# Where TensorE issues the last four attention products and the output projections of a round

## The chip, the cores and the metric

One core of one Trainium2 chip runs the whole program. The metric is the device time of one execution in microseconds, the median of the runs. One execution was also recorded by the profiler; it lasted 3959.9 us from its first to its last instruction.

## The reference, cut to what matters

The program computes a macaron block on x of shape (8, 512, 256): half a local feed-forward stage (two layers), a global attention with 16 heads, and the local stage again. Each layer of the local stage is, for all 8 sequences:

```python
h = shift_token(x)
q, k, v = split(h @ wqkv)                  # 8 heads of 64
q, k = rotary_xpos(l2norm(q) * qs, l2norm(k) * ksc)
o = local_attention(q, k, v)               # windows of 128, own block and the one before
x = x + o @ wo
h = layernorm(shift_token(x)) * lg + lb
a, g = split(h @ w1 + b1)
x = x + (a * gelu(g)) @ w2 + b2
```

The change concerns only this part.

## The kernel before, in words

**Rounds.** A local stage is called twice (call 0 and call 1). A call has 16 rounds, one for each sequence in the first layer and then in the second. The global attention lies between the calls. Within a round each engine works through a list of steps in a fixed order, written out by hand: `PE_STEPS` for TensorE, `ACT_STEPS` for ScalarE, `DVE_STEPS` for VectorE, `POOL_STEPS` for GpSimd. An engine does its steps strictly in that order and waits on semaphores where a step needs another engine's result. A step with `-` belongs to the previous sequence, one with `+` to the next, so three sequences are interleaved. In the last round of a call the `+` steps fall away; in the first one the `-` steps do.

**TensorE's steps that matter here.** A sequence has eight units of two heads by two query blocks.

- `S0` to `S7` (L1480): scores of a unit, on 64 rows of the array.
- `T0` to `T7` (L1490): the turnings (transposes) of a unit's probabilities into banks TB.
- `A0` to `A7` (L1510): the product of turned probabilities and values of a unit, on 64 columns of the array. `A4` and `A5` fill one bank, `A6` and `A7` the other. `A4` and `A6` are 8 instructions, `A5` and `A7` are 12.
- `W0` to `W3` (L1366 to L1368, `psum<-wo_hi,oT_hi` and its two companions): output projection of one head pair, 12 instructions. `W2` needs the bank of `A4` and `A5` after ScalarE (`O2`, L802) and VectorE (`P2`, L1087) have read it, `W3` likewise `A6`, `A7`, `O3` and `P3`.
- `+q`, `+k`, `+v` (L1366 to L1368, `psum<-wqkv_hi,hT_hi` and companions): the next sequence's projections, 6 instructions a step. `+q0` needs `hT_lo` of VectorE (L1016).
- `+Q`, `+K` (L1469): turnings of the rotated q and k, 4 instructions each.
- `-g`, `-a`, `-w`: the previous sequence's feed-forward products.
- `n0`, `n1` (L1528): turnings of the normalised stream, then `g0`, `a0` and so on.
- `B` (L1427): 48 products with one column each that fold the layer norm's bias into `b1`. Only the first round of each layer in each call has it (four rounds in all). In such a round `+v0` waits until VectorE has added the result to `b1t` (its own step `B`, L977).

**VectorE between W3 and n0.** Its list reads `P3 f1 +rq2 x l B +rk2 +ss2 r +rk3 +rq3 j0 j1 nl0 nl1`. Step `x` (L1096) adds the output projection to the stream and needs all four `W`. `l`, `r` (L1104, L1109) take the statistics, `+rk2`, `+rk3`, `+rq3` (L1027, L1031) rotate q and k of the next sequence, `+ss2` (L1038) sums squares, and `j0`, `j1` (L1122) normalise into `nrm`, which `n0` and `n1` of TensorE need. `L6` (L1084) copies the turned probabilities of unit 6 and frees the bank for `T7`; in the second layer VectorE has two further additions (`F`, L1147) ahead of it.

**Queues.** SyncE issues the DMAs in a fixed order too; the three shift copies of a round (L490 to L492) follow half of step `x`.

Of the kernel before, what the change touches and what calls it, by code (L numbers as in the profile page):

```python
# [14 lines left out]
B, N, D = 8, 512, 256  # L15
# [23 lines left out]


PE_STEPS = ("S0 -a2 -g3 S1 -w0 -g4 S2 -a3 -w1 S3 T0 -w2 T1 -a4 S4 T2 A0 S5 A1 A2 S6 T3 -w3 S7 T4 A3 -w4 +z0 +z1 "
            "-g5 A4 T5 +q0 +k0 A5 T6 -w5 +k1 +q1 T7 W0 +q2 A6 W1 A7 W2 +Q0 W3 B +K0 +k2 +v0 +K1 +Q1 +k3 +q3 +v1 "
            "+Q2 +v2 +v3 n0 n1 +Q3 g0 a0 g1 +K2 a1 g2 +K3").split()


# [1628 lines left out]
```

## Time and profile before

| | |
|---|---|
| median of 3 runs | 3955.74 us (3955.32 to 3961.43) |
| the profiled execution | 3959.9 us |
| TensorE matmul busy | 3751.7 us (95%), 23552 instructions |
| VectorE busy | 2649.7 us (67%) |
| ScalarE busy | 2237.8 us (57%) |
| GpSimd busy | 2192.4 us (55%) |
| mean granted TensorE clock | 0.985 of full |
| TensorE's share of the chain that ended last | 86% |

Busy times of TensorE are modelled from start to end of each matmul, and neighbours overlap. So the distance from one start to the next is the better measure of what a group of matmuls costs. The rows of the trace that matter are in a section of their own below; a row gives start, duration, engine, line, operation, what it writes and reads, and how often it repeats, with the idle time before it in brackets.

### The profile page before, as it was taken

To read this page: it belongs to the slowest core of one execution; us is meant where nothing else is said; L and a number is where in the kernel's file an instruction comes from. 1 tells how busy PE (TensorE), PEld (TensorE's weight loads), DVE (VectorE), ACT (ScalarE), POOL (GpSimd) and SP (SyncE) were. 2 spreads that over 40 slices of the span, in tenths; PEclk is the share of its full clock that TensorE was granted. 3 is DMA by queue.
4 is the path that set the end of the run, shared out by engine and by line. 5 is a ranking of instruction groups with operands and counts; after the bars stand their busy time and mean duration, and the time that the engine had idled before them with its cause. 6 is when DMAs were issued, how large, how long until landed. Compare 5 with 4: busy or idle time off the path is not lost.

```text
span 3959.9 us, 75575 instructions
## 1 busy us (share of the span) xinstructions
PE 3751.7 (95%) x23552; PEld 3069.5 (78%) x23552; DVE 2649.7 (67%) x7350; ACT 2237.8 (57%) x5232; POOL 2192.4 (55%) x2179
## 2 busy tenths in 40 slices
PE   4999999999999799999999999998999999999997
PEld 3777777777777688888888888886777777777776
DVE  6677777777777465555555555656777777767774
ACT  2666665567656455444444444445656765567564
POOL 3465565555555355555555555654555555555553
PEclk8999999999999899999999999999999999999999
DMA  4000001110010100000000010001010011100110
GB/s 142 16 31 28 19 19 53 48 36 24 30 31 29 46 28 22 1 17 7 12 17 2 17 44 1 17 1 52 20 35 22 19 41 50 39 30 24 34 32 25
DMA packets 119063, 114.72 MB, mean 29 GB/s; under 512 B 13181, under 2 KB 116233, under 8 KB 118793
## 3 DMA queue, kind: packets, MB, share of 16 engines
q1 hardware_dynamic: 118792, 111.44, 8.9%
q8 instruction: 131, 2.15, 0.2%
q14 instruction: 140, 1.14, 0.1%
HBM read 73.69 MB, written 29.36 MB: 26 GB/s over the span
## 4 chain that ended last, share of the span: by engine, by line
PE 86%; DVE 6%; issue 3%; ACT 2%; POOL 1%; DMA 1%; DVEq 0%; SPq 0%; ACTq 0%; POOLq 0%
PE psum L1366 21%; PE psum L1367 20%; PE psum L1368 20%; PE psum L1480 6%; PE psum L1490 5%; PE psum L1510 4%; PE psum L1469 3%; PE psum L1615 3%; PE psum L1563 1%; DVE probs L1065 1%; PE psum L1446 1%; PE psum L1427 1%; DVE turned_sin L1031 1%; DVE nT_lo L1127 1%; DVE ssq L1038 1%
## 5 line engine op out<-in xcount | busy, mean ns | idle before, releaser
L685 POOL TENSOR_TENSOR ge_lo<-ge,ge_hi 128x512 fp32r<-128x512 f32 x512 | 716.8, 1403 | 541.2 <-PE psum L1368 311.3
L885 ACT ACTIVATE ge<-psum 128x512 f32<-128x512 f32 x512 | 306.3, 598 | 623.7 <-PE psum L1615 611.8
L645 POOL TENSOR_SCALAR probs<-probs,rz 128x256 f32<-128x256 f32 (+1 forms) x1024 | 446.1, 456 | 354.6 <-DVE rz L1079 354.6
L1256 DVE CAST ge_hi<-ge 128x512 fp32r<-128x512 f32 x512 | 245.2, 480 | 537.5 <-ACT ge L885 531.4
L791 ACT ACTIVATE probs<-probs,nb,rq 128x256 f32<-128x256 f32 (+1 forms) x1024 | 575.1, 564 | 20.2 <-DVE nb L1073 17.1
L1065 DVE CUSTOM_DVE_ANT_0 probs<-psum,mask 128x256 f32<-128x256 f32 (+1 forms) x1024 | 339.3, 387 | 255.0 <-PE psum L1480 200.2
L627 POOL TENSOR_TENSOR rinv<-ssq,minus_half 128x16 f32<-128x16 f32 x124 | 376.1, 3033 | 126.6 <-DVE ssq L1042 123.2
L655 POOL TENSOR_TENSOR hid_lo<-gate,hid_hi 128x512 fp32r<-128x512 f32 x160 | 208.2, 1301 | 320.7 <-ACT hid_hi L823 320.7
L1366 PE MATMUL psum<-wqkv_hi,hT_hi 128*128 128x512 f32 x768 | 319.0, 415 | 5.9 <-DVE hT_lo L1016 3.4
L772 ACT ACTIVATE squares<-psum 128x512 f32<-128x512 f32 x256 | 153.2, 599 | 285.8 <-PE psum L1368 273.2
L622 POOL TENSOR_TENSOR turned_qk<-turned_qk,turned_sin 128x512 f32<-128x512 f32 x128 | 165.0, 1289 | 256.9 <-DVE turned_sin L1031 256.6
L1367 PE MATMUL psum<-wqkv_hi,hT_lo 128*128 128x512 f32 x768 | 306.8, 400 | 0.0
L1368 PE MATMUL psum<-wqkv_lo,hT_hi 128*128 128x512 f32 x768 | 306.7, 399 | 0.0
L1366 PE MATMUL psum<-nT_hi,w_hi 128*128 128x512 f32 x704 | 296.8, 422 | 9.3 <-DVE gate L1139 6.0
L1480 PE MATMUL psum<-kT,qT 64*128 64x256 f32 (+1 forms) x2048 | 269.9, 382 | 19.2 <-DVE mx L1065 16.4
L1366 PE MATMUL psum<-gw,w_hi 128*128 128x256 f32 x1024 | 287.4, 281 | 0.7 <-DVE gx L1281 0.7
L1367 PE MATMUL psum<-gw,w_lo 128*128 128x256 f32 x1024 | 287.6, 281 | 0.0
L1368 PE MATMUL psum<-gw,w_hi 128*128 128x256 f32 x1024 | 287.4, 281 | 0.0
L1490 PE MATMUL psum<-ident,probs 128*128 128x128 f32 x1792 | 252.0, 281 | 37.1 <-DVE pT L1084 17.6
L1367 PE MATMUL psum<-nT_hi,w_lo 128*128 128x512 f32 x704 | 279.2, 397 | 0.0
L1368 PE MATMUL psum<-nT_lo,w_hi 128*128 128x512 f32 x704 | 279.2, 397 | 0.0
L1490 PEld LDWEIGHTS psum<-ident,probs 128*128 128x128 f32 x1792 | 197.1, 143 | 103.0 <-issue 100.2
(163 smaller groups left out, 10650.0 us busy)
## 6 DMA issues: line engine op xcount, KB each, us to landing
xnext<-stream SPq DMA_DIRECT2D x32, 512.0 KB, 4.3
xmid<-stream SPq DMA_DIRECT2D x32, 512.0 KB, 3.8
stream<-xmid SPq DMA_DIRECT2D x16, 512.0 KB, 2.9
nrm<-xmid SPq DMA_DIRECT2D x32, 224.0 KB
wbuf<-L_ffn_wqkv SPq DMA_DIRECT2D x8, 768.0 KB, 8.2
wbuf<-L_ffn_w SPq DMA_DIRECT2D x8, 682.0 KB, 4.3
x_all<-L_attn_x SPq DMA_DIRECT2D x8, 512.0 KB, 7.6
stream<-x_all SPq DMA_DIRECT2D x8, 512.0 KB, 3.9
```

What stands on the lines that cost most here:

```text
L627: nc.gpsimd.tensor_tensor(rinv[:, i, :], ssq[:, i, :], minus_half[:], ALU.pow).then_inc(S["pool_r"], 1)
L645: last = nc.gpsimd.tensor_scalar(pu, pu, rz[:, h, t:t + 1], 1.0, ALU.mult, ALU.mult)
L685: nc.gpsimd.tensor_tensor(ges[1][:, k % 4, :], ge[:, k % 4, :], f32(ges[0][:, k % 4, :]), ALU.subtract).then_inc(S["g_lo"], 1)
L791: last = nc.scalar.activation(pu, pu, ACT.Exp, bias=nb[:, h, t:t + 1], scale=rq[:, 0, t, h:h + 1], accum_out=zs[:, h, t:t + 1])
L885: nc.scalar.activation(ge[:, k % 4, :], RB[k % 2], ACT.Exp, scale=GSCALE, accum_out=gz[:, h, t:t + 1]).then_inc(S["g_exp"], 1)
L1065: last = V.tensor_tensor_reduce(probs[:, i % 3, 2 * side + b, a:], RB[side][:, b * 2 * P + a:(b + 1) * 2 * P], mask[:, a:], 1.0, -3e38, AL ...
L1256: V.tensor_copy(ges[0][:, k % 4, :], ge[:, k % 4, :]).then_inc(S["g_hi"], 1)
L1366: mm(out_, lhs[0], rhs[0], start=start, stop=False, **kw)
L1367: mm(out_, lhs[1], rhs[0], start=False, stop=False, **kw)
L1368: return mm(out_, lhs[0], rhs[1], start=False, stop=stop, **kw)
L1480: last = mm(RB[side][:, b * 2 * P + a:(b + 1) * 2 * P], qT[rows, i // 2, t * P:(t + 1) * P], kT[rows, i // 2, (t - 1) * P + a:(t + 1) * P] ...
L1490: last = turn(TB[side][:, col * P:(col + 1) * P], probs[:, i % 3, 2 * side + t - blocks[0], a:a + P], ident[:])
```

## The change

Two lines of the list `PE_STEPS` change; no instruction is added or removed, and the other engines' lists stay.

```diff
-            "-g5 A4 T5 +q0 +k0 A5 T6 -w5 +k1 +q1 T7 W0 +q2 A6 W1 A7 W2 +Q0 W3 B +K0 +k2 +v0 +K1 +Q1 +k3 +q3 +v1 "
+            "-g5 T5 +q0 +k0 A4 A5 T6 -w5 +k1 +q1 T7 W0 +q2 W1 W2 A6 A7 +Q0 B +K0 +k2 W3 +v0 +K1 +Q1 +k3 +q3 +v1 "
```

`A4` goes behind `T5`, `+q0` and `+k0` and stands beside `A5`. `W1` and `W2` go ahead of `A6`, so that `A6` and `A7` stand together. `W3` goes behind `B`, `+K0` and `+k2`.

## Rows read from the trace of the kernel before

**Rows 1.** The page: busy time of TensorE; shares of the chain that ended last

```profile
PE 3751.7 (95%) x23552; PEld 3069.5 (78%) x23552; DVE 2649.7 (67%) x7350; ACT 2237.8 (57%) x5232; POOL 2192.4 (55%) x2179
...
PE 86%; DVE 6%; issue 3%; ACT 2%; POOL 1%; DMA 1%; DVEq 0%; SPq 0%; ACTq 0%; POOLq 0%
```

**Rows 2.** Timeline of TensorE, one first-layer round (start, duration, operation)

```profile
340.90 1.74 PE L1510 MATMUL psum<-pT,vs 128*64 128x128 f32 x20
...
353.49 0.87 PE L1510 MATMUL psum<-pT,vs 128*64 128x256 f32 x8
354.29 1.09 PE L1490 MATMUL psum<-ident,probs 128*128 128x128 f32 x8
355.14 0.48 PE L1366 MATMUL psum<-wqkv_hi,hT_hi 128*128 128x512 f32 x1
...
367.80 0.87 PE L1510 MATMUL psum<-pT,vs 128*64 128x256 f32 x8
368.60 0.38 PE L1366 MATMUL psum<-wo_hi,oT_hi 128*128 128x256 f32 x1
...
369.06 0.28 PE L1366 MATMUL psum<-wo_hi,oT_hi 128*128 128x256 f32 x1
...
369.41 0.28 PE L1366 MATMUL psum<-wo_hi,oT_hi 128*128 128x256 f32 x1
...
370.21 1.09 PE L1510 MATMUL psum<-pT,vs 128*64 128x128 f32 x12
371.23 0.38 PE L1366 MATMUL psum<-wo_hi,oT_hi 128*128 128x256 f32 x1
...
372.74 0.60 PE L1469 MATMUL psum<-ident,turned_qk 128*128 128x128 f32 x4
373.49 0.39 PE L1366 MATMUL psum<-wo_hi,oT_hi 128*128 128x256 f32 x1
...
375.00 0.60 PE L1469 MATMUL psum<-ident,turned_qk 128*128 128x128 f32 x4
375.35 0.48 PE L1366 MATMUL psum<-wqkv_hi,hT_hi 128*128 128x512 f32 x1
...
376.83 0.40 PE L1366 MATMUL psum<-wqkv_hi,hT_hi 128*128 128x512 f32 x1
...
386.61 0.66 PE L1528 MATMUL psum<-ident,nrm 128*128 128x128 f32 x4
```

**Rows 3.** Timeline of VectorE, the same round

```profile
353.63 0.69 DVE L1016 TENSOR_TENSOR hT_lo<-psum,hT_hi 128x512 fp32r<-128x512 f32 x1 [1.82 <-ACT hT_hi L764]
...
372.75 0.68 DVE L1087 TENSOR_TENSOR oT_lo<-psum,oT_hi 128x512 fp32r<-128x512 f32 x1
...
375.29 1.42 DVE L1096 TENSOR_TENSOR xmid<-psum,xmid 128x256 f32<-128x256 f32 x4 [0.57 <-PE psum L1368]
...
384.45 2.10 DVE L1122 TENSOR_SCALAR nrm<-xmid,mv,rs 128x128 f32<-128x128 f32 x4
```

**Rows 4.** Who waited for whom, whole run: total us, times, longest

```profile
PE psum L1528 <- DVE nrm L1122: 28.2, 31, 8.7
...
PE psum L1490 <- DVE pT L1084: 17.6, 14, 4.1
```

**Rows 5.** Timelines of VectorE and TensorE, one second-layer round

```profile
919.98 0.69 DVE L1027 TENSOR_TENSOR turned_qk<-psum,rope 128x512 f32<-128x512 f32 x1 [0.25 <-ACT squares L772]
...
927.64 1.09 PE L1490 MATMUL psum<-ident,probs 128*128 128x128 f32 x8 [1.07 <-DVE pT L1084]
```

**Rows 6.** First rounds of both layers, call 0: TensorE's timeline, then 769 to 778 by engine

```profile
135.82 4.79 PE L1427 MATMUL psum<-lnp,wbuf 128*128 128x1 f32 x48
...
767.55 0.39 PE L1366 MATMUL psum<-wo_hi,oT_hi 128*128 128x256 f32 x1 [1.82 <-DVE oT_lo L1087]
...
769.09 8.92 PE L1427 MATMUL psum<-lnp,wbuf 128*128 128x1 f32 x48
...
769.00:778.00 9.00, 9.00 (x51) 8.97 (x51) 3.60 (x12) 0.00 (x0) 0.00 (x0) 0.50 0.01 2
```

## The prediction

> **What bounds the kernel now.** I read the page first: TensorE is busy 95% of the span and carries 86% of the chain that ended last [rows 1]. That alone would say that whatever shortens TensorE's list shortens the run. So I went on to the timelines of TensorE and VectorE for a plain round, to see which of the two arrives last at each meeting point near the change. Two meeting points count. The first is `x`: VectorE has been idle for 0.57 us when the last `W3` product lets it start at 375.29 [rows 3]. The second is `n0`: `j0` on VectorE ends at 384.45 + 2.10 = 386.55, and TensorE starts `n0` at 386.61 [rows 2, 3]. TensorE's own work would have let it start at about 386.53 (the last of six `v3` products starts at 386.30 and such a product takes 0.235 to the next). So both arrive together, VectorE a hair later. The list of waits says the same of the whole run: TensorE waited for `nrm` 31 times, once a round [rows 4]. Between 375.29 and 386.55 VectorE is busy without a gap worth naming: 11.26 us of fixed work. So the round is really the loop `W3` → `x` → 11.26 us of VectorE → `n0` → rest of the list → `W3`. TensorE's matmuls between `W3` and `n0` just fit under the VectorE part. What decides is when the last `W3` product ends, and the change puts two steps ahead of `W3`.
>
> **The change, a plain first-layer round.** I follow the start of `W3` (373.49 before) and then its end [rows 2].
>
> *Ahead of `+q0`.* `A4` (353.49 to 354.29, 0.80) leaves this place. `T5` would start at about 353.40, since 0.09 of a step of entry to an attention product goes too, and take 0.79, so `+q0` could start at 354.19 and not at 355.14. But `+q0` needs `hT_lo`, which ends at 353.63 + 0.69 = 354.32 [rows 3]; with some 0.15 for the signal it starts at 354.47. Shift −0.67, and 0.28 us of the room won is a new wait. Behind this wait stand `+q0`, `+k0` and all else.
>
> *`A4` beside `A5`.* Apart, they take 0.80 and 1.02 from start to the next start (367.80 to 368.60, 370.21 to 371.23). Together they are 20 instructions: 1.74 busy at 340.90, less the 0.07 by which such a block overlaps its follower, 1.67. So `A5`'s 1.02 becomes 1.67: +0.65.
>
> *From `A6` to `Q0`.* Before: 367.80 to 372.74, 4.94. After: `W1`, `W2`, then `A6` and `A7` joined. Three steady products of `W` take 369.06 to 369.41 = 0.35, so twelve take 1.40. `W1` no longer follows an attention product (its first product was 0.10 longer), nor does `W2`, and only `W2` leads into one: entry costs 1.61 against 1.51 for a `W` that does not, 0.10 or 0.09. So 1.40 + 1.49 + 1.67 = 4.56, and the entry ahead of `A6` goes (−0.09): together −0.47.
>
> *From `Q0` to `W3`.* Before 0.75: `Q0` takes 0.35 like `K0` (375.00 to 375.35), and the rest is a wait for `P3`, which ends at 372.75 + 0.68 = 373.43 [rows 2, 3]. After: `Q0` 0.41 (turnings behind an attention product are 0.06 longer), `K0` and `+k2` 375.00 to 376.83 = 1.83: 2.24. The wait for `P3` is covered now; `A7` ends about 1 us later than before, `P3` at about 373.8, and `W3` starts after 374.5. Change +1.50.
>
> *Sum.* −0.67 + 0.65 − 0.47 + 1.50 = **+1.01** on the start of `W3`. `W3` itself follows a projection, not turnings: 1.40 for 1.51. Its end is **+0.91** late, so `x` is, and with VectorE's fixed 11.26 us so is `n0`. TensorE gets to `n0` early in spite of that: `W3` ends at 375.9 and stands before `+v0`, which is 0.9 earlier than the 376.83 of before. It then waits, for `rk2` (ahead of `+q3`), `rq3` (ahead of `+v3`) and `nrm`. The saving on TensorE (about 0.8 us a round) is real and is turned into waiting. I looked for cover: `T5` needs unit 5's probabilities and the copies of unit 4, and both are there over 1 us earlier; `W2` needs `P2` at about 367.8 and starts at 369.1. SyncE's three shift copies are issued off `x`, and move with it. GpSimd's steps move with VectorE's. No semaphore of the moved steps is past a DMA but that.
>
> **A second-layer round.** There `T7` waits 1.07 us for `L6` [rows 5], in 14 rounds [rows 4] (VectorE's list with `F`). TensorE's gains ahead of `T7` are lost; what counts is VectorE's chain `rq0` … `F` `-e` `L6`. It began 0.25 us late for the squares of `+q0` [rows 5]; with `+q0` 0.7 earlier this goes. I take −0.32 (bounds 0 and −0.4). Behind `T7` the terms are those above: −0.47 + 1.50 − 0.11 = +0.92. So **+0.60** a round.
>
> **Last rounds (two).** No `+` steps: `W3` follows `A7` at once and waits for `O3` and `P3`, two readings of 0.6 to 0.7 each with their signals (1.5 us), which `W2` had covered. Less the 0.6 saved: **+0.9** each.
>
> **First rounds of a layer (four).** `B` comes ahead of `W3`. It takes 4.79 at full clock and 8.92 at half clock; half clock was granted from 769 to 778, after TensorE had stood idle for 1.82 us ahead of `W3` [rows 6]. After the change `B` fills that idle time (a gain of about 1.8, and maybe of 4 if it runs at the full clock), but `W3`, `x` and `l` come behind it, and `+v0` then waits for VectorE's `B`, which stands behind `x` and `l`: 0.4 + 1.4 + 0.9 + 0.5, about 3.2 us in which TensorE stands still, and after that perhaps some time at half clock. I get about +2.5 in the first layer's and −1 in the second's, +3 in all; bounds −8 (`B` at full clock, no penalty) and +12.
> The Trainium skill, "TensorE: Matmul & The Clock Gate", section "What's actually happening", says that a TensorE that has been idle falls to half clock and has to earn the full clock back. The trace agrees in these rounds; by it the new wait ahead of `+v0` has a price beyond its length.
>
> **Total.** 14 first-layer rounds × 0.91 = 12.7; 12 second-layer rounds × 0.60 = 7.2; last rounds 1.8; first rounds 3. Sum +24.7 us. The profiled execution of 3959.9 would become 3984.6; it lay 4.2 above the median, so against 3955.7 the forecast is **3980**.
>
> **Rivals.**
>
> *Saving kept (faster).* VectorE's part from `x` to `n0` is not the bound, and TensorE's own time decides: 14 × −0.9, 12 × −1.2, plus 1.8 and 3, about −22: 3933. For it: TensorE's 86% of the chain [rows 1], and that `n0` was held by only some hundredths. Against it: `n0` starts 0.06 after `j0` ends, and the 11.26 us have no slack.
> The Trainium skill, "TensorEngine Tiling", section "Tiling Modes", says that a change of tiling mode drains TensorE; the change takes away four of eight such switches around `A4` to `A7`, and by that rule alone it wins. The rows agree that a switch costs: 0.15 for the exit and 0.09 for the entry. Chance 7%.
>
> *Delay absorbed (no change).* VectorE's part gets shorter, since `+k2` and `+k3` are there earlier and GpSimd and VectorE disturb each other less: `j0` takes 2.10 for four small operations, which leaves up to 1 us. Then 26 rounds × about +0.1, and 3964 or less; half of that cover gives 3968. Against it: GpSimd's steps move with VectorE's. 11% for the full one.
>
> *Worse (slower).* The wait ahead of `+v0` and half clock cost 5 us in each of four rounds and the −0.32 does not come: 3955.7 + 12.7 + 11 + 1.8 + 20 = 4001. 7%.
>
> *It does not do what it says.* If a block of 20 costs 1.82, as its parts, `W3` is 0.3 later still: 26 × 0.3 = 8 more, 3988. The row at 340.90 speaks against it. Inside my own case.
>
> **How the numbers follow.** My case has 75%: 3980, own range 3970 to 3990 (±0.2 on 26 rounds is 5, the first rounds give −8 to +9). With the half absorbed case the range is 3967 to 3990. A run of this kernel can be told from no change beyond about 0.2% (8 us). Faster 0.07, same 0.11, slower 0.82.
>
> **What the profile after would show.** Right: `n0` waits for `nrm` in nearly all rounds with TensorE idle ahead of it or ahead of `+q3` and `+v3`; the round's period is 0.9 and 0.6 longer; `x` starts 11.26 before `j0` ends; attention blocks of 20 at 1.74; a wait of 3 us ahead of `+v0` in four rounds. Wrong: no wait at `n0` and a shorter period (the first rival), or a VectorE part clearly under 11 us (the second).

## The result and the profile after

The changed kernel took 3984.0 us, median of 4 runs (3979.2 to 3988.6), against 3957.9 us (3955.3 to 3961.4) for the kernel before on the same chip: a ratio of 1.0059, 95% interval 1.0044 to 1.0074 (the quotient of the two medians is 1.0066). Slower, by some 23 us by the ratio and 26 by the medians. The profiled execution went from 3959.9 to 3977.5 us, +17.6; the working below is against these two executions. They understate the loss: the one of the kernel before was the slowest of its four runs (3961.4 as it was timed), the one of the changed kernel the fastest of its four (3979.2).

The page of the kernel after: busy time of each engine, and the shares of the chain that ended last.

```profile
PE 3744.6 (94%) x23552; PEld 3066.6 (77%) x23552; DVE 2646.9 (67%) x7350; ACT 2229.7 (56%) x5232; POOL 2192.0 (55%) x2179
...
PE 77%; DVE 13%; issue 5%; ACT 3%; POOL 2%; DMA 1%; DVEq 0%; ACTq 0%; SPq 0%; POOLq 0%
```

TensorE is busy 7 us less, and the run is 18 us longer. In the chain TensorE fell from 86% to 77% and VectorE rose from 6% to 13% [rows 1]: the end is now set through VectorE for a larger part.

TensorE's timeline of the kernel after, the round that answers to [rows 2] (start, duration, operation, idle before it):

```profile
355.23 1.03 PE L1490 MATMUL psum<-ident,probs 128*128 128x128 f32 x8
356.31 0.47 PE L1366 MATMUL psum<-wqkv_hi,hT_hi 128*128 128x512 f32 x1
...
359.27 1.74 PE L1510 MATMUL psum<-pT,vs 128*64 128x256 f32 x20
360.94 0.88 PE L1490 MATMUL psum<-ident,probs 128*128 128x128 f32 x6
...
365.86 1.04 PE L1490 MATMUL psum<-ident,probs 128*128 128x128 f32 x8
...
369.53 0.28 PE L1366 MATMUL psum<-wo_hi,oT_hi 128*128 128x256 f32 x1
...
372.42 1.74 PE L1510 MATMUL psum<-pT,vs 128*64 128x256 f32 x20
374.09 1.09 PE L1469 MATMUL psum<-ident,turned_qk 128*128 128x128 f32 x8
374.94 0.48 PE L1366 MATMUL psum<-wqkv_hi,hT_hi 128*128 128x512 f32 x1
...
376.43 0.28 PE L1366 MATMUL psum<-wo_hi,oT_hi 128*128 128x256 f32 x1
...
377.83 0.39 PE L1366 MATMUL psum<-wqkv_hi,hT_hi 128*128 128x512 f32 x1
...
385.24 0.66 PE L1469 MATMUL psum<-ident,turned_qk 128*128 128x128 f32 x4 [0.48 <-ACT qT L781]
386.08 0.50 PE L1366 MATMUL psum<-wqkv_hi,hT_hi 128*128 128x512 f32 x1 [0.18 <-DVE turned_sin L1031]
...
389.30 0.66 PE L1528 MATMUL psum<-ident,nrm 128*128 128x128 f32 x4 [0.15 <-DVE nrm L1122]
```

VectorE's timeline of the same round, the answer to [rows 3]:

```profile
378.12 1.42 DVE L1096 TENSOR_TENSOR xmid<-psum,xmid 128x256 f32<-128x256 f32 x4 [1.33 <-PE psum L1368]
...
380.36 0.68 DVE L1027 TENSOR_TENSOR turned_qk<-psum,rope 128x512 f32<-128x512 f32 x1
...
387.13 2.11 DVE L1122 TENSOR_SCALAR nrm<-xmid,mv,rs 128x128 f32<-128x128 f32 x4
```

Both attention blocks have 20 instructions and cost 1.67 to the next start (359.27 to 360.94, 372.42 to 374.09). From `T7` (365.86) to the start of `W3` (376.43) TensorE has no gap: 10.57 us, where it was 9.45 with a wait for `P3` in it. VectorE waits 1.33 us for the last `W3` product, where it waited 0.57. From the start of `x` to the end of `j0` it takes 11.12 us (378.12 to 387.13 + 2.11), and `n0` follows 0.06 later. Ahead of `n0` TensorE now stands still at three places (ahead of `Q2`, `v2` and `n0`, 0.48 + 0.18 + 0.15 = 0.81 us): the time it saved is there.

I use one measure from here on: the **period**, from one start of `n0` to the next, as the median over undisturbed rounds (6 of the first layer, 10 of the second). One period is the loop of the prediction: `n0` to `T7`, `T7` to `W3`, `W3` to `x`, `x` to the end of `j0`, and 0.06.

| us | before | after | change | forecast |
|---|---|---|---|---|
| period, first layer | 77.25 | 77.99 | +0.74 | +0.91 |
| period, second layer | 78.50 | 79.06 | +0.56 | +0.60 |
| `n0` to `T7` (the rest), first / second | 54.67 / 55.90 | 54.54 / 55.56 | −0.13 / −0.34 | −0.02 / −0.32 |
| `T7` to the start of `W3` | 9.45 / 9.48 | 10.57 / 10.62 | +1.12 / +1.14 | +1.03 |
| start of `W3` to `x` | 1.80 | 1.70 | −0.10 | −0.11 |
| `x` to the end of `j0` | 11.27 | 11.12 | −0.15 | 0 |

Added up over the profiled executions: the 26 plain rounds +16.7 us (forecast 19.9), the four first rounds, in order of time, +0.51, −1.37, +2.57 and −1.55, in all +0.2 (forecast 3), the two last rounds +0.14 and −0.19 (forecast 1.8), what follows the last `n0` +0.8. The reading of these against the forecast stands in the section on the points.

### The profile page after: what moved, and what is told of

The parts are those of the page before. It is cut to its first block, busy times and chain, and to the rows that moved or that the text cites. A ratio compares the mean times of both kernels' runs of the same rounds, so it can differ in the third digit from the quotient of the medians.

```text
span 3977.5 us, 75575 instructions
## 1 busy us (share of the span) xinstructions
PE 3744.6 (94%) x23552; PEld 3066.6 (77%) x23552; DVE 2646.9 (67%) x7350; ACT 2229.7 (56%) x5232; POOL 2192.0 (55%) x2179
## 3 DMA queue, kind: packets, MB, share of 16 engines
q14 instruction: 139, 1.14, 0.1%
## 4 chain that ended last, share of the span: by engine, by line
PE 77%; DVE 13%; issue 5%; ACT 3%; POOL 2%; DMA 1%; DVEq 0%; ACTq 0%; SPq 0%; POOLq 0%
PE psum L1366 19%; PE psum L1368 18%; PE psum L1367 18%; PE psum L1480 6%; PE psum L1490 5%; PE psum L1510 4%; PE psum L1615 3%; PE psum L1469 2%; DVE turned_sin L1031 2%; DVE nrm L1122 1%; PE psum L1563 1%; DVE ssq L1038 1%; DVE probs L1065 1%; DVE turned_qk L1027 1%; DVE xmid L1096 1%
## 5 line engine op out<-in xcount | busy, mean ns | idle before, releaser
L685 POOL TENSOR_TENSOR ge_lo<-ge,ge_hi 128x512 fp32r<-128x512 f32 x512 | 716.6, 1403 | 541.0 <-PE psum L1368 311.6
L655 POOL TENSOR_TENSOR hid_lo<-gate,hid_hi 128x512 fp32r<-128x512 f32 x160 | 208.1, 1301 | 322.5 <-ACT hid_hi L823 322.5
L772 ACT ACTIVATE squares<-psum 128x512 f32<-128x512 f32 x256 | 153.5, 600 | 378.5 <-PE psum L1368 217.4
L622 POOL TENSOR_TENSOR turned_qk<-turned_qk,turned_sin 128x512 f32<-128x512 f32 x128 | 165.5, 1293 | 278.6 <-DVE turned_sin L1031 278.4
```

Of the source, the lines that this page charges most:

```text
L685: nc.gpsimd.tensor_tensor(ges[1][:, k % 4, :], ge[:, k % 4, :], f32(ges[0][:, k % 4, :]), ALU.subtract).then_inc(S["g_lo"], 1)
```

## The experiments

Each run is compared with the kernel before, on the same chip. A diff shows only the stretch of a list that differs. Its `-` line is the kernel before, except where the text starts from the changed kernel; then it is the changed kernel. Unless a diff or the text says otherwise, the other engines' lists stay.

### One part of the change at a time

The whole change without the move of `W3`:

```diff
-T7 W0 +q2 W1 W2 A6 A7 +Q0 B +K0 +k2 W3
+T7 W0 +q2 W1 W2 A6 A7 +Q0 W3 B +K0 +k2
```

> The changed kernel with one part undone: W3 stands directly behind Q0 again, ahead of B, K0 and +k2. My theory (the end of W3 sets the round through VectorE's part from x to n0): A7 still ends about 1 us later than before, so P3 and with it W3 come about 0.45 us later than before in a first-layer round and 0.1 in a second-layer round, where T7 is 0.34 earlier. Sum 14 x 0.45 + 12 x 0.1 = 7 to 8 us over the kernel before (ratio 1.002), and about 15 us under the changed kernel. VectorE's part from x to the end of j0 is again 11.26 us. The rival, that TensorE's saving on switches counts in full: 26 x 0.8 = 21 us under the kernel before (0.995).

Measured: 3971.0 us, ratio 1.0023 (1.0013 to 1.0034); periods 77.52 and 78.58, `T7` to `W3` 9.79 and 9.84, `x` to `j0` 11.27. Putting `W3` back takes away more than half of the loss. The periods are 0.27 and 0.08 over the kernel before, where I had expected 0.45 and 0.1.

`A4` beside `A5`, and nothing else:

```diff
--g5 A4 T5 +q0 +k0 A5 T6
+-g5 T5 +q0 +k0 A4 A5 T6
```

> The kernel before with only A4 moved beside A5. My theory: in a first-layer round +q0 starts 0.67 us earlier and the block of 20 is 0.65 longer than A5, so T7 and W3 stay (period 77.25 as before); in a second-layer round L6 and so T7 and W3 come 0.34 earlier (period 78.16). Sum about 12 x 0.34 = 4 us under the kernel before (ratio 0.999). T5 is followed by a wait of 0.29 for hT_lo. The rival, that each join saves its switches (0.25 a round): 26 x 0.25 = 6 to 7 us under, spread over both layers alike.

Measured: 3957.0 us, ratio 0.9987 (0.9973 to 1.0002); periods 77.15 and 78.16. So this part gains 0.10 and 0.34 us a round; the total alone could not tell it from no change. It is the one part that keeps what it saves: it lies ahead of `T7`, and `T7` to `W3` stays as it was (9.44 and 9.48).

`W1`, `W2` ahead of `A6 A7`, and nothing else:

```diff
-W0 +q2 A6 W1 A7 W2 +Q0 W3
+W0 +q2 W1 W2 A6 A7 +Q0 W3
```

> The kernel before with only W1 and W2 put ahead of A6 and A7, W3 where it was. My theory: A7 ends about 1 us later, so O3, P3 and W3 come later; W3 about 0.45 us later in each of 26 plain rounds, period 77.7 and 78.95, sum 12 us over the kernel before (ratio 1.003). The rival, that the join saves its switches: 0.45 a round less, 12 us under (0.997).

Measured: 3978.3 us, ratio 1.0035 (1.0024 to 1.0046); periods 77.62 and 78.89. TensorE's timeline in this kernel:

```profile
375.80 0.66 PE L1469 MATMUL psum<-ident,turned_qk 128*128 128x128 f32 x4
377.36 0.38 PE L1366 MATMUL psum<-wo_hi,oT_hi 128*128 128x256 f32 x1 [0.90 <-DVE oT_lo L1087]
```

And its list of waits (total us, times, longest):

```profile
PE psum L1366 <- DVE oT_lo L1087: 35.2, 34, 2.2
```

Before, the same wait came to 7.9 us in 6 places on TensorE's matmuls. With only `Q0` (0.66 us) between `A7` and `W3`, the readings `O3` and `P3` are no longer covered: a wait takes the place of the saved switches, and more. The change avoids it by moving `W3`, which costs more still:

```diff
-+Q0 W3 B +K0 +k2
++Q0 B +K0 +k2 W3
```

> The kernel before with only W3 put behind B, K0 and +k2. My theory: W3 ends 1.3 to 1.4 us later, of which 0.14 comes back since +rk2 no longer waits for its squares; 1.2 a round in 26 plain rounds, about 31 us over the kernel before (ratio 1.008), more than the whole change costs. In the four first rounds of a layer a wait of about 3 us ahead of +v0. The rival, that W3 has room behind it: no change (1.000).

Measured: 3999.6 us, ratio 1.0093 (1.0076 to 1.0110); periods 78.56 and 79.84, `T7` to `W3` 10.98 and 11.04, `x` to `j0` 11.11. Alone, `W3`'s place costs 1.31 and 1.34 us a round. Comparing this run with the changed kernel gives what the joining saves: with `W3` late, joining all four products brings the periods from 78.56 and 79.84 back to 77.99 and 79.06, 0.57 and 0.78 us. So **the saving is real, but counts only where TensorE's own work is the last to arrive**, as between `T7` and a late `W3`.

### Where a joined block costs nothing

`A7` directly behind `A6`, but `W2` left behind it to cover the readings:

```diff
-W0 +q2 A6 W1 A7 W2 +Q0 W3
+W0 +q2 W1 A6 A7 W2 +Q0 W3
```

> The kernel before with only A6 put behind W1, beside A7 (W0 +q2 W1 A6 A7 W2 +Q0 W3). One switch into and out of attention products less, and A7 ends 0.4 us earlier than before. My theory: W3 waits for P3, and P3 waits for c1, so W3 stays where it was and its wait only grows by 0.35 us; period 77.25 and 78.5, no change (ratio 1.000). The rival, that the join saves its switches: 26 x 0.25 to 0.35 = 7 to 9 us under the kernel before (0.998).

Measured: 3965.7 us, ratio 1.0011 (1.0001 to 1.0020); periods 77.23 and 78.48, `T7` to `W3` 9.44 and 9.47, all as before. TensorE saves its switches and waits for `P3` instead: it stands still ahead of `W3` for 0.47 to 0.50 us in the undisturbed rounds, where it was 0.11 to 0.15. So the run is not faster; if anything it is a little slower. The next edit tests this: VectorE's residual `P3` ahead of `c1`, TensorE's list as before.

```diff
-P2 +rq1 L7 +c0 +c1 f0 P3 f1
+P2 +rq1 L7 +c0 P3 +c1 f0 f1
```

> The kernel before with TensorE's list untouched; only VectorE's list changes, P3 stands ahead of the second scaling of K (c1) instead of behind it. My theory: W3 loses its wait for P3 (0.39 us), and with it x, j0 and n0 come 0.35 earlier; TensorE has the same 0.35 ahead of it, so the period falls to 76.9 and 78.15 and the whole by 26 x 0.35 = 9 us (ratio 0.998). The rival, that the place of W3 in the loop does not matter or that TensorE's work is the bound by itself: no change.

Measured: 3934.5 us, ratio 0.9934 (0.9917 to 0.9950); periods 76.84 and 78.12, which is 0.41 and 0.38 shorter, as expected; TensorE no longer stands still ahead of `W3`. The total gain was 26 us where I had expected 9. In the profiled executions (−27.3) the plain rounds give 7.8 of it, and the rest lies outside them. In the two rounds that fold the second layer's bias the period fell from 90.21 and 90.43 to 83.34 and 85.46. There `P3` had stood behind `f0` (splitting a loaded weight, 1.76 us), and TensorE had waited 1.82 us ahead of `W3` [rows 6].

Part of this is the granted clock of the one execution and not the edit. With `W3` behind such a wait, but most of `B` at full clock, the same two rounds took 86.9 to 87.0 (in the kernels without the move of `W3`, with only `A4` moved, and with `W2` last alone). So some 3.3 us of each difference is the half clock that the kernel before happened to have there, and the last rounds (−1.3 and −1.5) are of that kind too, as shown further down. Among the runs on this chip with a mean granted clock of 0.988 the kernel before took 3956.3 us (one run) and this one 3934.3 to 3937.3, so about 20 us are left for the edit itself. In this run, TensorE's timeline where it does the second layer's `B`:

```profile
764.74 4.96 PE L1427 MATMUL psum<-lnp,wbuf 128*128 128x1 f32 x48
```

And VectorE's timeline of a plain round:

```profile
368.12 1.60 DVE L1048 TENSOR_TENSOR turned_qk<-turned_qk,rinv 128x512 f32<-128x512 f32 x1
370.63 0.69 DVE L1087 TENSOR_TENSOR oT_lo<-psum,oT_hi 128x512 fp32r<-128x512 f32 x1 [0.91 <-ACT oT_hi L802]
371.24 0.68 DVE L1048 TENSOR_TENSOR turned_qk<-turned_qk,rinv 128x512 f32<-128x512 f32 x1
...
373.48 1.42 DVE L1096 TENSOR_TENSOR xmid<-psum,xmid 128x256 f32<-128x256 f32 x4 [0.16 <-PE psum L1368]
```

`B` takes 4.96 us here and not 8.92. That agrees with my step "half clock behind the idle time", but it does not show it, and the other traces say less. In the kernel before, the first layer's `B` stands behind the same wait and runs at full clock (4.79, [rows 6]); its `W3` on TensorE's timeline:

```profile
134.31 0.38 PE L1366 MATMUL psum<-wo_hi,oT_hi 128*128 128x256 f32 x1 [1.75 <-DVE oT_lo L1087]
```

And TensorE's timeline of the kernel without the move of `W3`, first layer of call 1:

```profile
2727.78 0.38 PE L1366 MATMUL psum<-wo_hi,oT_hi 128*128 128x256 f32 x1 [2.21 <-DVE oT_lo L1087]
...
2729.30 4.78 PE L1427 MATMUL psum<-lnp,wbuf 128*128 128x1 f32 x48
```

Over the 13 kernels of this case, with four `B` each: behind a wait of 1.7 to 2.2 us ahead of `W3`, `B` took 8.92 in 8 of 20 rounds and 4.78 to 5.82 in the other 12. Without such a wait (none, or under 0.4 us) it never took 8.92: 4.78 to 6.94 in 32 rounds. So only behind the wait did a `B` run wholly at half clock, and not always there. Nor does taking the wait away keep the clock up: in all 44 rounds in which `B` began at full clock the granted clock fell to half 1.0 to 5.4 us after `B` had begun, though TensorE had not paused since. In this run it is at half from 769.1 to 772.4.

Both edits together (`W2` last, `P3` early):

> The last two edits together: A6 and A7 joined between W1 and W2 on TensorE, and P3 ahead of c1 on VectorE. My theory: both chains into W3 are shorter, the time from T7 to W3 falls from 9.45 to 8.7 us, and n0 comes 0.74 earlier; period 76.5 and 77.8, 26 x 0.74 = 19 us under the kernel before (ratio 0.995), more than the sum of the two alone. The rival, that such gains add: 0.35 a round, 9 us (0.998).

Measured: 3921.3 us, ratio 0.9897 (0.9881 to 0.9914); periods 76.47 and 77.75, so −0.78 and −0.75 as expected; `T7` to `W3` 8.70. The total is 39 us under the kernel before and not the 19 expected; as with `P3` alone, the rest lies outside the plain rounds. `W2` last brings nothing alone and 0.37 us a round once `P3` is early: then TensorE is the last to arrive at `W3`.

### The order of `B` and `W3`

The changed kernel, but `B` behind `W3`:

```diff
-+Q0 B +K0 +k2 W3
++Q0 +K0 +k2 W3 B
```

> The changed kernel with B moved behind W3 (Q0 K0 k2 W3 B). Plain rounds are as in the changed kernel (periods 78.0 and 79.05). In the four first rounds of a layer my theory has the wait of 3 us ahead of +v0 gone, since x and l run beside B; 2 to 3 us each less, 8 to 12 us under the changed kernel (ratio to the kernel before 1.003 to 1.004). The rival, that these rounds are set by something else (the half clock): no change against the changed kernel (1.006).

Measured: 3971.9 us, ratio 1.0033 (1.0019 to 1.0047), 10 to 12 us under the changed kernel, as expected. The plain periods (78.03, 79.09) are those of the changed kernel, the rounds with `B` are shorter. TensorE's timeline in the changed kernel, first round of the second layer:

```profile
770.71 5.92 PE L1427 MATMUL psum<-lnp,wbuf 128*128 128x1 f32 x48
...
780.04 0.41 PE L1366 MATMUL psum<-wo_hi,oT_hi 128*128 128x256 f32 x1
...
784.84 0.76 PE L1366 MATMUL psum<-wqkv_hi,hT_hi 128*128 128x512 f32 x1 [2.87 <-issue]
```

VectorE's, the same stretch:

```profile
782.01 1.42 DVE L1096 TENSOR_TENSOR xmid<-psum,xmid 128x256 f32<-128x256 f32 x4 [6.09 <-PE psum L1368]
783.39 0.17 DVE L1101 MEMSET nrm<- 1x128 f32 x1
783.49 0.85 DVE L1104 BATCH_NORM_STATS2 st<-xmid 128x6 f32<-128x128 f32 x4
784.25 0.15 DVE L977 TENSOR_TENSOR b1t<-b1t,psum 128x10 f32<-128x10 f32 x1
```

And TensorE's with `B` behind `W3`:

```profile
774.07 6.72 PE L1427 MATMUL psum<-lnp,wbuf 128*128 128x1 f32 x48
781.44 0.77 PE L1366 MATMUL psum<-wqkv_hi,hT_hi 128*128 128x512 f32 x1 [0.66 <-issue]
```

In the changed kernel VectorE's `B` (784.25) stands behind `x` and `l`, and `+v0` waits for it with nothing to do. With `B` behind `W3`, TensorE computes `B` while VectorE does `x` and `l`, and the wait falls from 2.87 to 0.66.

### Does `P3` matter when `W3` is late?

The changed kernel's TensorE list whole, with VectorE's `P3` ahead of `+c1` (VectorE's two lines of diff stand under "Where a joined block costs nothing"):

> The changed kernel's TensorE order whole, with VectorE's residual P3 ahead of c1. Theory (W3's place costs what it costs because the chain T7, W3, x, r, j0, n0 closes the plain rounds, and P3's early place takes c1 and f0 out of the same chain on VectorE): the two are different links of one chain and add up. Early P3 alone gave 0.9934, the change alone 1.0059, so ratio 0.999 to 1.000; the plain rounds' periods 0.4 us under the changed kernel's (77.6 and 78.7). Rival (behind W3's late place TensorE's own queue decides when x starts, so that an earlier P3 meets nobody who waits for it): periods stay at 78.0 and 79.05, ratio 1.003 to 1.006, with only the rounds that load a weight shorter.

Measured: 3982.8 us, ratio 1.0064 (1.0047 to 1.0081); periods 77.97 and 79.05, those of the changed kernel. **My theory fell and the rival held.** The same edit that gave 26 us before gives nothing here. VectorE's timeline shows why:

```profile
379.34 0.69 DVE L1087 TENSOR_TENSOR oT_lo<-psum,oT_hi 128x512 fp32r<-128x512 f32 x1 [1.95 <-ACT oT_hi L802]
...
382.56 1.42 DVE L1096 TENSOR_TENSOR xmid<-psum,xmid 128x256 f32<-128x256 f32 x4 [0.73 <-PE psum L1368]
```

VectorE had 1.33 us to spare ahead of `x` in the changed kernel. `P3` and `x` are not links that add up: `P3` runs beside TensorE's list, and only the later of the two holds `W3`.

### What is the last to arrive after that

`P3` early, `W2` last, and `A4` beside `A5`:

```diff
--g5 A4 T5 +q0 +k0 A5 T6 -w5 +k1 +q1 T7 W0 +q2 A6 W1 A7 W2
+-g5 T5 +q0 +k0 A4 A5 T6 -w5 +k1 +q1 T7 W0 +q2 W1 A6 A7 W2
```

> Early P3 and W2 last, as in the run with both, and in addition the change's own joining of A4 and A5 behind +k0. Theory: joining A4 and A5 gained 0.1 us a first-layer round and 0.34 us a second-layer round when it was alone, because it puts more projection work in front of T7's wait; the chain from T7 on is the same, so the gains add: 0.9897 less 0.0013, ratio 0.988 to 0.989, periods about 76.4 and 77.45. Rival (with P3 early the wait ahead of T7 is no longer where the second layer loses time): ratio 0.990, periods 76.5 and 77.8.

Measured: 3921.7 us, ratio 0.9913 (0.9896 to 0.9929); periods 76.35 and 77.43. The plain rounds gained 0.12 and 0.32, as expected, some 5 us over the run. The total doesn't show it: 3921.7 against 3921.3, on another chip. The ratio lies above the 0.988 to 0.989 that I had expected, and the rival's 0.990 lies within its interval. In the profiled executions only 1.9 of the 5 us were left; `n0` of round 0 came 1.5 later and the last round of call 1 took 71.91 where it had taken 70.53. The total is inconclusive; the periods (0.12 and 0.32 shorter, for the rival's 0) are not.

In this kernel `T7` still waits in the second layer, and VectorE waits earlier in the same stretch. The last edit moves the two additions of `-F` into that gap:

```diff
--y5 L5 +rq0 +rk0 +ss0 -F -e L6
+-F -y5 L5 +rq0 +rk0 +ss0 -e L6
```

> The run before this one (early P3, W2 last, A4 and A5 joined) with one more edit on VectorE: the step -F of the round before stands ahead of -y5 and L5 instead of behind ss0. Theory: in the second layer T7 waits 1.0 us for VectorE's last normalising step because -F stands between ss0 and L6; taken out of that stretch, the 14 plain second-layer rounds lose most of that wait, 0.7 to 1.0 us each, 10 to 14 us in all, ratio 0.985 to 0.986, second-layer period about 76.6, first-layer period unchanged. Rival (L5 and the two rk steps ahead of it are now late by as much, and T5 or T6 waits instead): ratio 0.988 to 0.989 or above, with TensorE's wait at T5 or T6.

Measured: 3906.0 us (3904.9 to 3909.0), ratio 0.9874 (0.9857 to 0.9890), the fastest kernel here, 15.6 us under the run before it. The second layer's period fell from 77.43 to 76.35, the first layer's stayed (76.37). `T7` on TensorE, then the gap on VectorE, without the last edit:

```profile
910.90 1.09 PE L1490 MATMUL psum<-ident,probs 128*128 128x128 f32 x8 [0.84 <-DVE pT L1084]
```

```profile
901.98 0.74 DVE L1139 SCALAR_TENSOR_TENSOR hid_r<-psum,b1t,gate 42x512 f32<-42x512 f32 x1 [1.13 <-ACT gate L817]
```

The same two views with it:

```profile
911.43 1.04 PE L1490 MATMUL psum<-ident,probs 128*128 128x128 f32 x8
```

```profile
902.31 1.33 DVE L1147 SCALAR_TENSOR_TENSOR xmid<-xmid,nrm 128x512 f32<-128x512 f32 x2
903.56 0.73 DVE L1139 SCALAR_TENSOR_TENSOR hid_r<-psum,b1t,gate 42x512 f32<-42x512 f32 x1
```

The 1.33 us of `-F` fill the 1.13 us in which VectorE had waited for `gate`. The ratio is 0.001 to 0.002 above what I expected, since that was counted from the run with both edits; against its own predecessor the gain is 15.6 us for an expected 10 to 14, and 1.08 us a plain second-layer round (there are 12, not the 14 of my expectation). The rival fell: in all 12 of them TensorE has no wait at `T5`, `T6` or `T7`; the 0.84 us at `T7` are gone.

## Why the prediction was right, point by point

**What bounds the kernel: right.** That the parts of the loop add up to the period is no evidence, since they must. The evidence is that two of its links hold still: `n0` follows `j0` by 0.06 in every kernel that was run, and `x` to `j0` has only two values, to 0.01 (11.27 and 11.12), by where `W3` stands. What the edits change is the start of `W3` against `T7`, or `T7` against `n0`, and the period follows. TensorE's share of 86% in the chain would have given the wrong sign. TensorE's new waits stand ahead of `+Q2` (for ScalarE's copy of q), `+v2` and `n0`; I had named `+q3`, `+v3` and `nrm`, so one of three places was right.

**Ahead of `+q0`: right, on a round that was not typical.** `T5` to `+q0` is 1.08 (355.23 to 356.31), 0.79 of work and 0.29 of the new wait; expected 0.28. But the round of [rows 2] had a period of 77.06 and not 77.25: in it `+q0` stood 0.82 us behind the end of the first half of `hT_lo`, in the undisturbed rounds 0.92. There the changed kernel has 0.97 from `T5` to `+q0`, so a wait of 0.18, and `+q0` starts 0.77 earlier for my 0.67.

**`A4` beside `A5`: right.** 1.67 to the next, twice. In the second layer `n0` to `T7` came out at −0.34 for −0.32. In the first layer it was −0.13 for −0.02; the missing 0.10 is that of `+q0` above.

**`A6` to `Q0`, `Q0` to `W3`: mis-sized by 0.1.** `W1` and `W2` took 2.89 (1.40 + 1.49) and the block 1.67, as worked out. `+k2` took 1.49. The miss is in the turnings behind the block: I gave `Q0` and `K0` 0.41 + 0.35 = 0.76, and they took 0.85 (374.09 to 374.94). The price stood in my own rows: eight turnings behind an attention product, 354.29 to 355.14 in [rows 2], also 0.85.

**VectorE's fixed 11.26: mis-sized by 0.15.** It became 11.12. In both traces I can place it: from the start of `x` to `+rk2` it was 2.38 (375.29 to 377.67) and is 2.24 (378.12 to 380.36). All kernels with `W3` behind `+k2` have 11.11 to 11.13, all with `W3` ahead of it 11.26 or 11.27. So it belongs to `W3`'s place, and is a small part of the rival "delay absorbed": 0.15 of 0.91. The profile names no wait this short, but the starts show one: with `W3` ahead of `+k2`, `+rk2` starts 0.03 us after ScalarE has finished its squares (L772) in all 16 undisturbed rounds, and with `W3` behind it the squares are done 3.14 us earlier than that step.

**First rounds: right in kind, with sizes that one execution can't settle.** The wait ahead of `+v0` is there in all four (2.86 to 2.87), 3.14 us from the start of the last `W3` product (781.70) to `+v0` (784.84) for an expected 3.2, and the idle time ahead of `W3` is gone. The half clock behind the new wait is there in all four as well: the first product of `+v0` takes 0.76 us at 784.84. Layer 1 gave +0.51 and +2.57 (forecast 2.5 each), layer 2 −1.37 and −1.55 (−1 each). In layer 1 that includes loading and the global attention, which end before the moved steps; from `T7` to `n0` the four rounds gave +1.90, −1.31, +2.06 and −1.39, in all +1.3. `B` took 5.92, between its 4.79 and 8.92 [rows 6]. I had read [rows 6] as "idle, therefore half clock", and that was too strong, as the count over 13 kernels above shows. The granted clock alone can move such a round by more than any of these four changes: from `T7` to `n0` the second layer's first round took 35.25 us in the kernel before and 32.04 in the one with only `A4` moved, whose steps from `T7` on are the same.

**Last rounds: wrong in their total.** The wait that I named is there, on TensorE's timeline of the kernel after, the last round of call 0:

```profile
1330.79 1.74 PE L1510 MATMUL psum<-pT,vs 128*64 128x256 f32 x20
1333.94 0.38 PE L1366 MATMUL psum<-wo_hi,oT_hi 128*128 128x256 f32 x1 [1.41 <-DVE oT_lo L1087]
```

But before, the same stretch was not at full clock, which I hadn't looked up. First TensorE's timeline of the kernel before, then its windows (stretch, length, busy time of the five engines, granted clock, DMA share, GB/s):

```profile
1318.13 0.37 PE L1366 MATMUL psum<-wo_hi,oT_hi 128*128 128x256 f32 x1
...
1320.61 1.53 PE L1510 MATMUL psum<-pT,vs 128*64 128x256 f32 x8
1322.06 0.39 PE L1366 MATMUL psum<-wo_hi,oT_hi 128*128 128x256 f32 x1
```

```profile
1318.00:1322.00 4.00, 4.00 (x24) 3.15 (x22) 0.61 (x2) 1.07 (x2) 0.00 (x0) 0.57 0.55 154
```

`W0` took 2.48 and `A6` 1.45 there, for some 1.5 and 0.80 at full clock. In the changed kernel the granted clock is 1.00 from 1306 to 1334. So two differences cancel: `T7` to `W3` is 8.68 us where it was 8.90, and would have been about 7.3. The 7.3 are measured: 7.32 in the kernel with only `W3` moved, whose last rounds have the order of the kernel before and were at full clock there. The term by itself was some +1.4, more than my +0.9. The half clock comes and goes there without a change of the work: in the kernel with `W2` last alone, the two last rounds took 70.52 and 71.92.

**The rivals.** "Saving kept" fell at `n0`, where VectorE still arrives last. "Worse" fell, since the −0.34 came and the first rounds cost next to nothing in all. "A block of 20 costs 1.82" fell (1.67).

The sum is thus 17.6 in the profiled executions, for 24.7: 3.2 less in the plain rounds, 2.8 in the first and 1.9 in the last, and 0.8 more at the end.

**Luck in the number.** That the median (3984.0, 26 us over the kernel before) lies so near the forecast 3980 is in part luck. The plain rounds, which the argument is about, give 16.7 of the forecast 19.9; what brings the medians to 26 no profile shows, since none was taken of a median run; rounds whose granted clock changes from run to run are the likely place. Shown are the sign, the loop and its links, and the periods to 0.2 us.

## What to carry to other kernels

Where engines work through fixed lists, find the loop that repeats and take its period apart at the places where they meet; a busy share of 95% says nothing of which of two engines that arrive within 0.1 us of each other sets the period. An instruction group that is made cheaper pays only on the side of a meeting point that arrives last, so ask first who arrives last there, and move that one; here one step moved on VectorE gave more than everything that was done to TensorE's list. Read rows in a round whose period is the usual one, and compare the granted clock before a difference outside the plain rounds is put down to the edit. Don't put other work ahead of the step that a slower engine waits for, however full it keeps your own engine.

## What the runs showed of the hardware

- Between attention products (64 columns of the array) and full-width ones a switch costs about 0.15 us on leaving and 0.09 on entering, more than one attention product. `A4` to `A7` in four blocks took 0.80 and 1.02 each, together 3.64 a round; in two blocks of 20 they took 3.34, so each joining saved 0.15, besides the entry.
- VectorE's `+c0` and `+c1` (L1048, 128x512, both operands in SBUF) took 1.6 us each before. With `P3` between them, the second took 0.68, and the median of all 128 fell from 1.59 to 0.69 us; VectorE's busy time fell by 29.5 us over the run. The traces show what goes with it: GpSimd's operations of the same size (L618, L622, L655, L685). In the kernel before, each of the 88 slow ones (1.32 to 1.78) runs beside one for at least 0.76 us, and none of the 40 fast ones (0.67 to 0.74) for more than 0.52. With `P3` early 58 are slow and 70 fast, by nearly the same bounds. On the path it made no difference that could be seen: the kernel with the late `W3` and `P3` early has it as well, and its periods stayed. VectorE's timeline and GpSimd's, a plain round of the kernel before:

```profile
369.53 3.30 DVE L1048 TENSOR_TENSOR turned_qk<-turned_qk,rinv 128x512 f32<-128x512 f32 x2
```

```profile
369.30 1.28 POOL L622 TENSOR_TENSOR turned_qk<-turned_qk,turned_sin 128x512 f32<-128x512 f32 x1
370.54 1.74 POOL L618 TENSOR_TENSOR turned_qk<-turned_qk,turned_sin 128x512 f32<-128x512 f32 x1
```

- 48 matmuls of one column kept TensorE busy without a gap, and yet the granted clock fell to half 1.0 to 5.4 us after the first of them in all 44 rounds that began them at full clock. Behind an idle time of 1.7 to 2.2 us a few steps earlier they ran wholly at half clock (8.92 us) in 8 of 20 rounds, without it in none of 32.
